# Value and receptance projections as seven quarter products in a fused recurrent-attention and gated-MLP kernel

## The reference, cut to what matters

```python
x_prev = pad(x[:, :-1])                              # token before
xk = x * time_mix_k + x_prev * (1 - time_mix_k)      # xv and xr likewise
k, v = xk @ W_k.T, xv @ W_v.T                        # 256 x 256 weights
r = sigmoid(xr @ W_r.T)
wkv = wkv_scan(k, v, time_decay, time_first)         # recurrence over tokens
x = x + (r * wkv) @ W_o.T
h = silu(x' @ w1.T * s1) * (x' @ w2.T * s2)          # x' = layernorm(x), 256 -> 1024
h = gelu(h @ h1.T * sh1)                             # 1024 x 1024
h = gelu(h @ h2.T * sh2)                             # 1024 x 1024
x = x + h @ w3.T * s3                                # 1024 -> 256
```

## Time and profile before

| what | value |
|---|---|
| median of three runs | 1473.9 us |
| time of the profiled execution | 1469.84 us |
| its span in the profile | 1468.1 us |
| PE busy | 1459.3 us (99%) |
| DVE busy | 1136.9 us (77%) |
| ACT busy | 997.9 us (68%) |
| POOL busy | 99.6 us (7%) |
| granted PE clock | 1.00 of full speed |

### The profile page before, as it was taken

The page is one execution under the profiler, slowest core; times in us unless marked ns, Lnnn a source line. Parts: engine busy times, 40 slices in busy tenths (PEclk is TensorE's granted clock), DMA queues, the critical chain, the costliest instruction groups (busy, mean ns, idle before and its releaser), DMA issues.

```text
span 1468.1 us, 28022 instructions
## 1 busy us (share of the span) xinstructions
PE 1459.3 (99%) x10236; PEld 1314.6 (90%) x10236; DVE 1136.9 (77%) x1600; ACT 997.9 (68%) x1525; POOL 99.6 (7%) x128
## 2 busy tenths in 40 slices
PE   8999999999999999999999999999999999999999
PEld 7989898998989989898898989989899898998998
DVE  6786878778797786977868788687877869778655
ACT  7995665767657576675856757676576765757655
POOL 1112000010100101001010010100001010010100
PEclk9999999999999999999999999999999999999999
DMA  9988574755737467375674746657475674746654
GB/s 345 386 296 282 171 246 120 239 170 194 251 113 258 142 201 250 123 255 145 202 225 149 247 132 219 195 173 252 121 245 152 206 245 120 262 136 203 186 184 133
DMA packets 105374, 300.02 MB, mean 204 GB/s; under 512 B 10496, under 2 KB 41856, under 8 KB 103552
## 3 DMA queue, kind: packets, MB, share of 16 engines
q1 hardware_dynamic: 97184, 291.75, 58.4%
q0 software_dynamic: 8160, 7.87, 4.3%
HBM read 265.44 MB, written 33.09 MB: 203 GB/s over the span
## 4 chain that ended last, share of the span: by engine, by line
PE 97%; ACT 1%; DVE 1%; issue 0%; DMA 0%; POOL 0%; DVEq 0%; SPq 0%; ACTq 0%; POOLq 0%
PE acc L713 27%; PE acc L715 27%; PE att L606 11%; PE acc L687 7%; PE acc L688 7%; PE acc L739 4%; PE acc L741 4%; PE att L645 4%; PE acc L844 2%; PE acc L842 2%; PE att L585 1%; PE att L688 1%; PE att L687 1%; PE acc L813 1%; ACT early L1246 0%
## 5 line engine op out<-in xcount | busy, mean ns | idle before, releaser
L713 PE MATMUL acc<-op_hi,ring 128*128 128x256 f32 x3360 | 810.3, 286 | 0.5 <-issue 0.5
L715 PE MATMUL acc<-op_lo,ring 128*128 128x256 f32 x3360 | 788.5, 279 | 0.0
L713 PEld LDWEIGHTS acc<-op_hi,ring 128*128 128x128 f32 x3360 | 631.0, 188 | 18.6 <-issue 17.6
L715 PEld LDWEIGHTS acc<-op_lo,ring 128*128 128x128 f32 x3360 | 632.2, 188 | 11.1 <-issue 10.0
L1716 DVE TENSOR_TENSOR op_lo<-blocks,op_hi 128x1024 fp32r<-128x1024 f32 (+2 forms) x271 | 339.4, 1268 | 66.5 <-ACT op_hi L1111 60.2
L1111 ACT ACTIVATE op_hi<-blocks 128x1024 fp32r<-128x1024 f32 (+2 forms) x263 | 284.5, 1093 | 111.9 <-DVE blocks L1711 68.6
L687 PE MATMUL acc<-x_hi,w_rnd 128*128 128x512 f32 x420 | 167.1, 398 | 0.3 <-DVE blocks L1702 0.3
L688 PE MATMUL acc<-x_lo,w_rnd 128*128 128x512 f32 x420 | 166.1, 396 | 0.0
L1151 ACT ACTIVATE blocks<-acc,vec 128x256 f32<-128x256 f32 x268 | 104.9, 476 | 68.2 <-PE acc L715 60.9
L1151 ACT ACTIVATE blocks<-parts,vec 128x256 f32<-128x256 f32 x240 | 101.1, 498 | 64.1 <-DVE parts L1774 61.5
L1107 ACT ACTIVATE fresh<-acc,vec 128x512 f32<-128x512 f32 x105 | 72.1, 686 | 74.8 <-PE acc L688 74.8
(11 more groups left out here) (216 smaller groups left out, 1904.7 us busy)
## 6 DMA issues: line engine op xcount, KB each, us to landing
ring<-scratch SPq DMA_DIRECT2D x426, 512.0 KB, 4.2
scratch<-stage SPq DMA_DIRECT2D x11, 1024.0 KB, 12.2
stage<-in_w_ffn SPq DMA_DIRECT2D x10, 1024.0 KB, 10.7
x_in<-in_x SPq DMA_DIRECT2D x32, 256.0 KB, 4.6
out<-x_next SPq DMA_DIRECT2D x30, 256.0 KB, 4.4
out<-mix_v POOLq DMA_DIRECT2D x30, 256.0 KB, 4.2
mix_r<-in_x_T SPq DMA_DIRECT2D x14, 512.0 KB, 5.7
norm<-norm_rows SPq DMA_DIRECT2D x14, 512.0 KB, 4.4
```

Of the source, the lines that this page charges most:

```text
L713: pe.matmul(out, act(w), act(op_hi[:, k, c, :]), start=(begins and c == 0 and m % 2 == 0), stop=False, skip_group_check=True)
L715: mm = pe.matmul(out, act(w), act(op_lo[:, k, c, :]), start=False, stop=(c == QC - 1), skip_group_check=True)
```

## The change

Two by two blocks of weights A (output by input channels) and of inputs b (channels by tokens, a quarter being 128 channels by 256 tokens) are multiplied in seven products in place of eight, for v (`w = 0`) and for r (`w = 1`). `project` keeps k alone. The new parts are:

- On POOL, once, before the loop: `sum_mixing` scales W_v by 0.25, and makes four weight sums for both matrices, in a buffer laid over a spare weight slot.
- On DVE, in each pass: `quad_inputs` makes four differences of quarters in three instructions that each wait for the one before (128x512, 128x256, 128x256), and `quad_sums` adds one product to two others (128x512 from PSUM). Both are done for v and for r.
- On PE, in each pass: `project_part` does 2, 2, 2 and 1 products of 128x256, four parts each for v and r, with halves of steps between.
- On ACT, in each pass: `again` copies a partial sum from one place in PSUM to another (two copies of 128x256) and one product to SBUF (128x256), `copy_quads` copies two results (128x512). They replace `copy_kvr` for v and r.

```diff
+            def project_part(t, w, part):
+                src, sums = quarters(QUADS[w][0]), quarters(QUADS[w][1])
+                T_1, T_3, T_2, T_4 = (sums[:, k, :] for k in range(4))
...
+                if part == 0:
+                    pe.wait_ge(mix_sums, 5)
+                    pe.wait_ge(dve_quad.sem, dve_quad.at(t, 2 * w + 1))
+                    pe.wait_ge(WHOLE.act_kvr.sem, WHOLE.act_kvr.at(t, 2 * w + 2))
+                    product(w, Q11, a11, src[:, 0, :], start=True)
+                    pe_part.add(product(w, QT3, S_3, T_3, stop=True))
+                elif part == 1:
+                    pe.wait_ge(act_again.sem, act_again.at(t, 2 * w + 1))
+                    product(w, Q11, a12, src[:, 2, :], stop=True)
+                    pe_part.add(product(w, Q21, S_2, T_2))
+                elif part == 2:
+                    pe.wait_ge(WHOLE.act_kvr.sem, WHOLE.act_kvr.at(t, 2 * w + 3))
+                    product(w, Q21, a22, T_4, stop=True)
+                    WHOLE.pe_kvr.add(product(w, Q22, S_1, T_1))
+                else:
+                    pe.wait_ge(dve_quad.sem, dve_quad.at(t, 2 * w + 2))
+                    WHOLE.pe_kvr.add(product(w, Q22, S_4, src[:, 3, :], stop=True))
...
-                    project(WHOLE, i + 1, [0, 1, 2])
+                    project(WHOLE, i + 1, [0, 1])
                     step(i, 0, 2, [0])
+                    project_part(i + 1, 0, 0)
                     step(i, 0, 2, [1])
-                    project(WHOLE, i + 1, [3])
-                    step(i, 0, 3)
-                    step(i, 0, 4)
+                    project_part(i + 1, 0, 1)
+                    step(i, 0, 3, [0])
+                    project_part(i + 1, 0, 2)
+                    step(i, 0, 3, [1])
+                    step(i, 0, 4, [0])
+                    project_part(i + 1, 0, 3)
+                    step(i, 0, 4, [1])
                     step(i, 0, 5)
-                    project(WHOLE, i + 1, [4])
-                    step(i, 0, 6)
+                    project_part(i + 1, 1, 0)
+                    step(i, 0, 6, [0])
+                    project_part(i + 1, 1, 1)
+                    step(i, 0, 6, [1])
+                    project_part(i + 1, 1, 2)
                     step(i, 1, 0, [0])
-                    project(WHOLE, i + 1, [5])
+                    project_part(i + 1, 1, 3)
                     step(i, 1, 0, [1])
...
+            def again(t, w, k):
+                if k == 0:
+                    act.wait_ge(pe_part.sem, pe_part.at(t, 2 * w + 1))
+                    act_again.add(act.activation(Q21, Q11, ACT.Copy))
+                else:
+                    act.wait_ge(pe_part.sem, pe_part.at(t, 2 * w + 2))
+                    WHOLE.act_kvr.add(act.activation(Q22, Q21, ACT.Copy))
+                    act_again.add(act.activation(QUADS[w][2][:, 0, 0:SEG], QT3, ACT.Copy))
...
+            def quad_inputs(t, w):
...
+                link(WHOLE, dve.tensor_tensor(T[:, 0:2, :], b[:, 1::2, :], b[:, 0:2, :], ALU.subtract))
+                settle(WHOLE, t)
+                link(WHOLE, dve.tensor_tensor(T[:, 2, :], b[:, 3, :], T[:, 0, :], ALU.subtract))
+                settle(WHOLE, t)
+                dve_quad.add(dve.tensor_tensor(T[:, 3, :], b[:, 2, :], T[:, 2, :], ALU.subtract))
+
+            def quad_sums(t, w):
+                dve.wait_ge(WHOLE.pe_kvr.sem, WHOLE.pe_kvr.at(t, 2 * w + 3))
+                dve.wait_ge(act_again.sem, act_again.at(t, 2 * w + 2))
...
```

More of the change, by code:

```diff
@@ L146, in build @@
     X_AFTER = 19
-    DVE_EXTRA = 4
+    DVE_EXTRA = 0
     BLOCK = 32
@@ L286, in build, with quarters, by_half @@
         out_tok = mix_v[:].rearrange("p c t -> p (c t)").rearrange("p (b d) -> p b d", b=NB)
+        quad = [att[:, SEG * k:SEG * (k + 1)] for k in range(4)]
+        Q11, QT3, Q21, Q22 = quad
+        QUADS = ((mix_v, r_sb, v_sb), (mix_r, mix_v, r_sb))
+        def quarters(t):
+            return t[:].rearrange("p c (n t) -> p (c n) t", n=n_seq)
         def by_seq(ap):
             return ap.rearrange("p c (n t) -> p c n t", n=n_seq)
+        def by_half(ap):
+            return ap.rearrange("p (n t) -> p n t", n=n_seq)
         def by_block(ap):
@@ L371, in build @@
         dve_rows = tally("dve_rows", 1, 1, ahead=-2)
+        dve_quad, act_again, pe_part = (tally(n, k, 1, ahead=-2) for n, k in (("dve_quad", 4), ("act_again", 4), ("pe_part", 4)))
+        mix_sums = ctx.enter_context(nc.semaphore("mix_sums"))
         ld_norm = tally("ld_norm", 1, 16, ahead=-2)
@@ L608, in project, with product @@
                     s.pe_kvr.add(mm)
+            def product(w, bank, weights, moving, start=False, stop=False):
+                return pe.matmul(bank, weights, moving, start=start, stop=stop, skip_group_check=True)
+            def project_part(t, w, part):
+                src, sums = quarters(QUADS[w][0]), quarters(QUADS[w][1])
+                T_1, T_3, T_2, T_4 = (sums[:, k, :] for k in range(4))
+                a11, a12, a22 = (wm[:, 1 + w, c, e * P:(e + 1) * P] for e, c in ((0, 0), (0, 1), (1, 1)))
+                S_1, S_2, S_3, S_4 = (w_sums[:, w, k, :] for k in range(4))
+                if part == 0:
[15 more added lines that the diff above has]
+                    WHOLE.pe_kvr.add(product(w, Q22, S_4, src[:, 3, :], stop=True))
             def project_late(which):
@@ L1068, in receptance @@
                 act.wait_ge(s.act_kvr.sem, s.act_kvr.at(t))
+                if not isinstance(t, int):
+                    act.wait_ge(dve_quad.sem, dve_quad.at(t, 4))
                 s.act_exp.add(act.activation(r_sb[:, :, s.cols], r_sb[:, :, s.cols], ACT.Tanh, scale=0.5))
@@ L1393, in _ @@
                 share(WHOLE, i + 1)
+                again(i + 1, 1, 0)
                 g12(i, 0)
                 g22(i, 0)
+                again(i + 1, 1, 1)
                 hiB22(i)
                 hiT1(i)
-                copy_kvr(WHOLE, i + 1, [4])
                 g21(i, 0)
+                copy_quads(i + 1, 1)
                 hiT23(i)
@@ L1600, in exponents @@
                 distance(s, t)
+                if not isinstance(t, int):
+                    quad_sums(t, 0)
                 settle(s, t)
@@ L2015, in _ @@
                 lo23(i, 1)
+                quad_inputs(t, 0)
                 t23(i, 1)
@@ L2024, in _ @@
                 lo6(i)
+                quad_inputs(t, 1)
                 loB11(i)
@@ L2031, in _ @@
                 t23b(i)
+                quad_sums(t, 1)
                 loT1(i)
@@ L2121, in next_deviation, with sum_mixing @@
                 deviation(WHOLE, t, dve_var.sem, dve_var.at(t, 2), pool_rstd.add, (next_var, next_mean), (next_norm[:, 0:NB], next_norm[:, NB:2 * NB]))
+            def sum_mixing():
+                pool.wait_ge(WHOLE.pe_kvr.sem, WHOLE.pe_kvr.at(1))
+                pool.tensor_scalar(wm[:, 1, :, :], wm[:, 1, :, :], 0.25, None, ALU.mult).then_inc(mix_sums, 1)
+                pool.wait_ge(mix_sums, 1)
+                pool.wait_ge(pe_half.sem, pe_half.at(0, PLAIN_STEPS))
+                a11, a12, a21 = (wm[:, 1:3, c, e * P:(e + 1) * P] for e, c in ((0, 0), (0, 1), (1, 0)))
+                a22 = wm[:, 1:3, 1, P:2 * P]
+                s1_, s2_, s3_, s4_ = (w_sums[:, :, k, :] for k in range(4))
+                pool.tensor_tensor(s1_, a21, a22, ALU.add).then_inc(mix_sums, 1)
+                pool.tensor_tensor(s3_, a11, a21, ALU.subtract).then_inc(mix_sums, 1)
+                pool.wait_ge(mix_sums, 3)
+                pool.tensor_tensor(s2_, s1_, a11, ALU.subtract).then_inc(mix_sums, 1)
+                pool.wait_ge(mix_sums, 4)
+                pool.tensor_tensor(s4_, a12, s2_, ALU.subtract).then_inc(mix_sums, 1)
             def hi_plain(l, row, s):
@@ L2178, in _ @@
             next_deviation(1)
+            sum_mixing()
             add_out(0, (0, 1))
```

27 lines of the change are left out of this document (20 added, 7 removed).

## The result

| | before | after |
|---|---|---|
| median of 4 runs, us | 1474.68 (1470.48 to 1475.95) | 1530.45 (1526.85 to 1531.68) |
| profiled execution, us | 1469.84 | 1531.68 |
| its span, us | 1468.1 | 1530.0 |
| TensorE's granted clock over the span | 1.000 | 0.992 |

The account below looks back on a forecast made before the run. PE's own work, laid end to end, was taken to bound the kernel. Stalls of 4.16 us a pass less 0.86 saved give 3.30, over fourteen passes 46.2 us: median 1473.9 to 1520 us, range 1500 to 1537.

Parts of the forecast that it names:

- the case called likeliest: All four waits of PE form in each pass, giving 1520 us; chance 62%.
- What PE saves: PE, v and r: 14 products of 0.43 us replace four outputs of 1.72, saving 0.86 us a pass.
- First wait: Step 2 of layer 1 waits for p1, delayed on ACT by DVE's differences: stall 2.31 us a pass.
- Second wait: Step 6 waits for c22 on DVE, covered only by part 0 of r: stall 0.79 us a pass.
- Third wait: Part 2 of r waits for ACT's copy behind table load and gelu: stall 0.41 us a pass.
- fourth: Part 3 of r waits for quad_sums on DVE, behind T2 and T3: stall 0.65 us a pass.
- The restart: PE goes on 0.24 us after a release, range 0.15 to 0.30, at each of four waits.
- take its 0.86 back: Rival: the waits find their covers and PE saves 0.86 us a pass, 1462 us; chance 5%.
- the two late waits: Rival: the waits ahead of parts 2 and 3 of r, 1.06 us together, don't form, 1505 us; chance 16%.
- the table load has no drain: Rival judged: ACT's table load carries a drain of some 1.38 us a pass, 1539 us; chance 2%.
- no saving: Rival: single products among fp32r steps cost PE 0.86 us more a pass, 1532 us; chance 8%.
- a wait in layer 2: Rival: a further wait on T2 or its first product's copy adds 0.5 to 1 us a pass, 1527 to 1534; 7%.

Follow-up runs that it names:

- experiment 7: Kernel of Experiments 6 with the last half of step 5 and first of step 6 ordered by column block, so one PSUM bank completes earlier; 1461.20 us, ratio 0.9923.
- Experiment 1: The changed kernel with p1 on ACT moved ahead of the second rounded copy; 1488.86 us, ratio 1.0110.
- experiment 2: The kernel before, keeping its eight block products, with DVE also making the three input differences for v, unused; 1490.20 us, ratio 1.0112.
- Experiments 6: Kernel of Experiment 5 with layer 1's c22 made by DVE in two halves, step 6 waiting for each where needed; 1466.71 us, ratio 0.9964.
- Experiment 5: The changed kernel with p1 early and three more ACT moves, so B12's gelus no longer stand behind a PE product; 1473.22 us, ratio 1.0004.
- experiments 3: The changed kernel with the first difference of v done three times, lengthening the gap ahead of step 2; 1564.17 us, ratio 1.0610.
- experiment 4: The changed kernel with the two small differences of v moved behind t23(i, 1), shortening the gap ahead of step 2; 1506.53 us, ratio 1.0224.
- experiment 8: Kernel of experiment 2 with its first difference done five times, a long gap without the new products; 1556.33 us, ratio 1.0574.

## Why the prediction was right, and what it lacked

The direction was right and 1530.45 lies in the range, but the case called likeliest gives 1520. By the prediction's own steps:

- **What PE saves**, 0.86 a pass: right in the main. The changed products take their forecast 0.43 each, and without waits experiment 7 has 0.75 of it in the pass. The 0.11 that are missing aren't explained.
- **First wait**, 2.31: right. From 351.92 (348.49 and eight records of 0.429) to 354.14 is 2.22, and the next record comes 0.08 later than usual behind the first one, 2.30 in all. The rows of ACT:

```profile
351.54 1.06 ACT L1177 ACTIVATE op_hi<-blocks 128x1024 fp32r<-128x1024 f32 x1 [3.95 <-DVE blocks L1802]
352.50 0.58 ACT L1097 ACTIVATE k_sb<-att 128x512 f32<-128x512 f32 x1
352.98 1.02 ACT L1208 ACTIVATE acc<-acc 128x1024 f32<-128x1024 f32 x1
```

  The rounded copy starts 3.05 us behind the k output (348.49), where it was 1.53 in the earlier trace rows: 1.52 later, forecast 1.5. Experiment 1 takes the wait away by ACT's order alone. But that there was "0.9 spare" ahead of it was only half the truth: experiment 2 shows that the k copy ahead of it, for the third output, had 0.2.
- **Second wait**, 0.79: right. It is 0.83: 0.59 of idle time, the drain of 0.17, and 0.08 in the next record. Experiments 6 and 7 take it away.
- **Third wait**, 0.41, was too large, and the **fourth**, 0.65, too small. The rows of a pass of the changed kernel, on PE:

```profile
660.28 0.27 PE L757 MATMUL acc<-op_lo,ring 128*128 128x256 f32 x1
660.47 0.70 PE L626 MATMUL att<-mix_v,wm 128*128 128x256 f32 x2
661.01 0.59 PE L626 MATMUL att<-mix_v,w_sums 128*128 128x256 f32 x2
...
663.21 0.28 PE L757 MATMUL acc<-op_lo,ring 128*128 128x256 f32 x1
664.09 0.70 PE L626 MATMUL att<-mix_r,w_sums 128*128 128x256 f32 x2 [0.60 <-DVE r_sb L1635]
```

  and on ACT:

```profile
655.55 1.28 ACT L1217 ACT_TABLE_LOAD   x1
656.84 3.31 ACT L1217 ACTIVATE blocks<-parts,vec 128x256 f32<-128x256 f32 x8
660.06 0.36 ACT L1107 ACTIVATE att<-att 128x256 f32<-128x256 f32 x1
```

  Part 2 starts at 660.47, 0.05 after ACT's copy ends (660.42); it is late by 0.07 in its start and 0.11 in its first record, 0.18 in all. The walk had the copy end 0.17 behind PE's asking, and it ended 0.02 behind it (660.40); and it added a restart of 0.24, which was 0.16 here. What it didn't wait, part 3 waits: it starts 0.88 behind the record before it in place of 0.12, and its next record 0.11 later again, 0.87 in all. The two make 1.05; forecast were 1.06. The sum of both was right because both hang on one run of ACT, which began late at 655.16. Experiment 5 shows that run as the cause. The load takes 1.28, and gelu starts 0.01 behind it. The drain that the Trainium skill (ScalarE: Activation LUTs, What ACT_TABLE_LOAD costs) adds to a load, about 1.38 us, isn't there on either side: ACT's copy ends 0.02 before the load (655.53 to 655.55).
- **The restart**, 0.24: a little large, and part of its reading was wrong. That the record at 718.90 was 0.43 long shows no wait, as the one behind it in the kernel before starts on time (an output of 1.72 and a record of 0.12 behind 717.33):

```profile
719.17 0.28 PE L715 MATMUL acc<-op_lo,ring 128*128 128x256 f32 x1
```

  Start and next record together, a restart costs 0.22 for steps (first and second wait) and 0.15 to 0.16 for the fp32 parts of r (third and fourth).
- **The sum**: 4.16 of waits forecast, 2.30 + 0.83 + 0.18 + 0.87 = 4.18 measured; 3.30 more a pass forecast, 3.37 measured in the eight short passes.
- **What was missing** is a term. The prediction priced four waits by their lengths, and took PE's pace behind them as given. It is not: 5 stretches x 1.63 = 8.2 us come from the clock. That is half of the 15.7 us between the forecast for the profiled execution (1516) and its 1531.68; 0.9 are the 13 passes' 0.07, 2.4 the first pass, 4.2 run-in and end. Experiments 1, 3, 4 and 8 show that the slow stretches go with the length of the wait. Whether the first pass, run-in and end have to do with the change isn't shown.

The rivals fell: PE didn't take its 0.86 back; the two late waits are there with 1.05 together; the saving is there; no gap stands in layer 2; and the table load has no drain. But the time alone doesn't say so. 1530.45 lies nearer to two of the rivals (1532 for no saving, 1527 to 1534 for a wait in layer 2) than to the likeliest 1520, and the range reached so far up for causes that weren't there. It is the pass of 92.89 us and the list of waits that show the mechanism; that the clock's 8.2 us, for which the prediction had no term, stayed inside the range was luck.

## What to carry to other kernels

When one engine is busy to 99% and its program has waits with little spare, a saving on it is worth nothing until each engine that feeds it has been walked in order: here 4.2 us of waits came for the 0.86 us that were to be saved. They lay in the order of the work and not in the new products: 3.4 us went with ACT's order alone (92.89 to 89.50), and the rest with c22 in halves and PE's own order at one place (to 88.77). Look for the wait that was nearly late already; moving one consumer's copy ahead of other work (p1) gave back three quarters of the loss. And TensorE's longest wait may cost more than its length, as the one of 2.06 us did here in five passes of 13, so take that one away first.

## What the runs showed of the hardware

- After a wait of TensorE the granted clock can fall to the lower of its two levels: 0 of 28 times behind 1.1 us of idle time (experiments 2 and 4), 5 of 13 behind 2.06, 14 of 14 behind 3.4 to 3.5, 13 of 14 behind 3.9 to 4.0. It lasts 3.4 us in most cases and then costs 1.6 us (94.52 - 92.89; 95.4 - 93.8 in experiment 8); two times each in experiments 3 and 8 it lasted 6.8 us.
- The length isn't all of it. The single wait of 2.3 us at the gate had slow records behind it in the changed kernel and in experiment 5, and none in experiment 4. Between 34 and 38 us, in the run-in, the clock fell behind a wait of only 1.36 us in the changed kernel and 1.48 in experiment 5, and it did not behind 1.67 in experiment 8. What picks these, and the five of 13 among equal waits, stays open.
- The fall may come after the restart: at 354.14 PE went on at full speed for a microsecond, and only then slowed.
- An fp32 product starts 0.05 us behind the end of the ACT copy or DVE sum that released it (660.42 to 660.47, 664.03 to 664.09), and the record after it is 0.11 late. A step's first product starts 0.14 us behind the end of its release (354.00 to 354.14 for p1), and the record after it is 0.08 late.
